# Attention stage: the seven identity-by-identity products left out of every step in which the whole pipeline runs

## The reference, cut to what matters

```python
x = x + 0.5 * ffn(layernorm(x), gate_w, w1, w2, w3)
x = x + attention(layernorm(x), Wq, Wk, Wv, Wb, conv_q_w, conv_k_w, conv_v_w, rms_w, Wo)
x = x + 0.5 * ffn(layernorm(x), gate_w, w1, w2, w3)
```

```python
A = I + tril(Kb K^T, -1);  T = inverse(A);  W = T Kb;  U = T Vb
mid = U - W S^T
O = Q S^T + (Q K^T * M) mid
S = S + mid^T K
```

## Time and profile before

| | |
|---|---|
| median of three runs | 1484.42 us |
| the profiled execution | 1485.0 us, span 1483.3 us |
| TensorE (PE) busy | 1339.8 us, 90% of the span |
| VectorE (DVE) busy | 1080.7 us, 73% |
| ScalarE (ACT) busy | 888.6 us, 60% |
| GpSimd (POOL) busy | 791.0 us, 53% |
| mean granted TensorE clock | 0.952 of 2.4 GHz |

### The profile page before, as it was taken

The page is one execution under the profiler, slowest core; times in us unless marked ns, Lnnn a source line. Parts: engine busy times, 40 slices in busy tenths (PEclk is TensorE's granted clock), DMA queues, the critical chain, the costliest instruction groups (busy, mean ns, idle before and its releaser), DMA issues. The chain is left out here.

```text
span 1483.3 us, 48601 instructions
## 1 busy us (share of the span) xinstructions
PE 1339.8 (90%) x17442; PEld 1229.8 (83%) x17442; DVE 1080.7 (73%) x3189; ACT 888.6 (60%) x2096; POOL 791.0 (53%) x1485
## 2 busy tenths in 40 slices
PE   7867999998579999999999999999999838999997
PEld 7766999998468888888878888888887628999997
DVE  6774556555577888999998998998998455555554
ACT  4434556664356777767677767677675324555663
POOL 3672333334355557567776677676866550333334
PEclk9998999999689999999999999999999768999999
DMA  9833433330011122222222222222222353333320
GB/s 265 244 123 105 124 94 94 96 89 12 22 19 42 41 51 47 66 55 75 68 65 72 58 73 75 66 73 68 67 73 47 103 175 104 100 94 91 91 76 17
DMA packets 191382, 123.11 MB, mean 83 GB/s; under 512 B 101531, under 2 KB 182951, under 8 KB 191152
## 3 DMA queue, kind: packets, MB, share of 16 engines
q1 hardware_dynamic: 167200, 77.68, 21.1%
q0 software_dynamic: 14976, 33.93, 6.6%
q10 hardware_dynamic: 8976, 8.40, 1.9%
HBM read 69.71 MB, written 57.55 MB: 86 GB/s over the span
## 5 line engine op out<-in xcount | busy, mean ns | idle before, releaser
L504 PE MATMUL ffn_both<-ws,ffn_xhi 128*128 x1472 | 252.7, 283 | 0.1
L728 DVE SCALAR_TENSOR_TENSOR ffn_hid<-ffn_both,ffn_xb,ffn_sil 128x128 f32<-128x128 f32 x368 | 103.7, 344 | 199.8 <-ACT ffn_sil L858 194.7
L1727 DVE SCALAR_TENSOR_TENSOR raw_w<-attn_raw,taps,raw_w 128x256 f32<-128x256 f32 x576 | 239.3, 482 | 4.6 <-ACT raw_w L2140 4.5
L858 ACT ACTIVATE ffn_sil<-ffn_both,ffn_xb 128x128 f32<-128x128 f32 x368 | 104.9, 368 | 189.0 <-PE ffn_both L504 189.0
L504 PEld LDWEIGHTS ffn_both<-ws,ffn_xhi 128*128 128x128 f32 x1472 | 211.1, 191 | 0.4 <-issue 0.3
L930 POOL DMA_INDIRECT out_dram<-ffn_xb,ffn_to x92 | 90.4, 983 | 167.3 <-PE ffn_both L504 112.9
L930 POOL DMA_INDIRECT x_after_first<-ffn_xb,ffn_to x92 | 90.5, 984 | 163.4 <-PE ffn_both L504 107.9
L2416 POOL TENSOR_TENSOR attn_inv<-attn_inv,attn_term 64x14 f32<-64x14 f32 (+6 forms) x448 | 138.5, 309 | 35.1
L528 PE MATMUL ffn_pos<-ws,ffn_hhi 128*128 x736 | 153.8, 292 | 2.0 <-DVE ffn_xb L741 2.0
L504 PE MATMUL ffn_both<-ws,ffn_xlo 128*128 x736 | 149.2, 285 | 0.0
L1326 PE MATMUL attn_fr<-attn_xhi,wqkv 128*128 128x256 f32 x768 | 139.9, 291 | 4.5 <-ACT attn_bth L2147 2.5
(11 more groups left out here) (333 smaller groups left out, 3532.0 us busy)
## 6 DMA issues: line engine op xcount, KB each, us to landing
ffn_xb<-listed_rows SPq DMA_DIRECT2D x184, 130.5 KB, 2.2
attn_xin<-x_after_first ACTq DMA_DIRECT2D x32, 256.0 KB, 2.7
attn_xres<-x_after_first SPq DMA_DIRECT2D x32, 256.0 KB
x_after_attention<-attn_xres SPq DMA_DIRECT2D x32, 256.0 KB
attn_xg<-x_after_attention SPq DMA_DIRECT2D x32, 256.0 KB, 3.4
ffn_xb<-in_L_attn_x_dram SPq DMA_DIRECT2D x7, 1024.0 KB, 6.7
raw_w<-in_L_ffn_w_dram SPq DMA_DIRECT2D x8, 512.0 KB, 8.8
small_blocks<-raw_w SPq DMA_DIRECT2D x256, 8.0 KB
```

What stands on the lines that cost most here:

```text
L504: last = pe.matmul(hp[k % 2][:, j, e], (xhi, xlo)[b][:, k % 2, q, j * P:(j + 1) * P], ws[:, bass.ds(experts[2 * j + e], 1), a, q].rearrang ...
L728: last = dve.scalar_tensor_tensor(hid[:, k % 2, j, e], hp[k % 2][:, j, e, HF:], xw[k % NW][:, j, DM + 3 + e:DM + 4 + e], sil[:, j, e], ALU ...
L858: last = act.activation(sil[:, j, e], hp[k % 2][:, j, e, 0:HF], ACT.Silu, scale=xw[k % NW][:, j, DM + 3 + e:DM + 4 + e])
L1727: dve.scalar_tensor_tensor(acc[:, j, r], raw[:, j, r, :, tap:tap + P], taps[:, j, r, tap:tap + 1], acc[:, j, r], ALU.mult, ALU.add)\
```

## The change

```diff
-            def x_turn(f):
+            def x_turn(f, s):
                 m = f[0]
                 wait(pe, vtok_ready, m)
-                keep_busy(fr[:, 0, 0:P], 3)
+                if not s:
+                    keep_busy(fr[:, 0, 0:P], 3)
                 pe.wait_ge(xn_ready, m + 1)
...
                 if f:
-                    x_turn(f)
+                    x_turn(f, s)
...
                 if f:
                     beta_turn(f)
-                    fill(f)
+                    if not s:
+                        fill(f)
                 if t:
                     second_products32(t)
```

## The result

The changed kernel takes 1490.67 us in the median of 20 runs (1481.31 to 1503.23) and the kernel before 1483.83 us in 20 runs of the same comparison (1477.13 to 1488.47): ratio 1.0052, 95% interval 1.0034 to 1.0069. It is slower, by about 7 us; the forecast was 1494, in the range 1482.5 to 1502.

A forecast was written before the change was run, and what follows sets the result against it. A step is bound by a closed round passing from engine to engine, not TensorE alone. 11.2 us lost to half speed less 1.5 gained is +9.7 on 1485.0, 1494.7; as a median 1494 us, range 1482.5 to 1502.

The forecast's parts named there:

- The round: Full steps: a closed round passes from engine to engine; the cut identity products stand in TensorE's two pauses.
- x_turn, 1.5 us gained: Three products before the transposes of x: 0.25 us gained in six steps behind `positions`, 0 elsewhere; bounds 0 and 4.2.
- the number forecast: Second Gram product, L1388 before the change: would wait for VectorE's L1767 in about twelve steps.
- fill, worth 0 as time: Four products before L1461: cutting leaves TensorE empty 1.2 us in each of 29 steps, no instruction earlier.
- The clock: Behind fill's pause: 3.4 us at 1.2 GHz in some steps, beginning 2 to 4 us behind L1461.
- 0.45 + 1.34 us for a fall: Extra time at half speed on L1605 (0.45) and L1614 (1.34), 1.8 us if both fell in.
- 8 falls at 1.4 us: Half-speed stretches in 8 of 29 full steps, 1.4 us each (bounds 1.0 and 1.7): 11.2 us lost.
- bounds of 4 and 14: Number of half-speed stretches in 29 steps: from one step in seven (4) to one in two (14).
- No fall: Rival: transposes and small products hold the clock at 2.4 GHz in the full steps; 1483 us, chance 0.26.
- a fall in every step: Rival: half speed behind the thin stretch in all 29 steps, +39 us, 1524 us; chance 0.06.
- The faster case: Rival: TensorE is the bound; 0.7 us from x_turn in each of 29 steps, 1464 us; chance 0.04.
- the second rival: Full steps: half speed in every one, 1524 us, as if transposes did not count for the clock; chance 0.06.

The follow-up runs named there:

- Run 1: Only the three x_turn products left out of the full steps, fill kept, against the kernel before: 1502.70 us, ratio 0.9985.
- run 2: Only the four fill products left out of the full steps, x_turn's kept, against the kernel before: 1519.69 us, ratio 1.0089.
- run 3: The changed kernel with eight identity transposes in fill's place, timed against the kernel before: 1502.59 us, ratio 0.9981.

## Why the prediction held, step by step

**The round.** Right. The cuts made no step shorter by their own length: TensorE's busy time fell by 40 us and the plain steps without a fall stayed at 23.37 us where they had 23.35 to 23.36. One reading of the round was incomplete: the prediction says that VectorE waits for L1416 and for little else, but in the same stretch it also waited 20.9 us, 23 times, for ScalarE's `squares` (L2162), nearly as long as the 22.5 us for L1416. That wait is part of the same round, and no term hangs on it.

**x_turn, 1.5 us gained.** Right in place and, within what can be told, in size. L1320 now waits for ScalarE's L2110 in 23 steps, 0.8 us at most, and L1389 waits for VectorE in 12 steps, the number forecast. The steps with `positions` at their end fell from 24.0 us or more to between 23.37 and 23.65, and the next ones rose by up to 0.25 (steps with a fall left aside). Run 1 gives the net: 2.0 us of the stretch.

**fill, worth 0 as time.** Right: 1.14 to 1.19 us of pause in most steps, no instruction earlier. The longest is 2.3 us, where a transfer was late by 1.1.

**The clock.** Right in cause and sign, not in the place within the step. The prediction had half speed begin 2 to 4 us behind L1461 and L1614 take over 2.5 us; it began 0 to 1.1 us behind, and L1615 took 1.99 to 2.68 us, over 2.5 in one of the six. What it slowed is L1606, L1507 and the small products before L1615: from L1462 to L1615 it is 3.1 to 3.5 us in these steps in place of 2.25. Of the prediction's 0.45 + 1.34 us for a fall the first came in five of the six, in whole or in part, and of the second at most half; the rest of the cost came from L1507 and the small products, which the sum had not counted.

Forecast were 8 falls at 1.4 us, 11.2 us. There were 6. The six steps with a fall, against the same kind of step without one (25.63 less 23.5, 25.01 less 23.4, 24.80 less 23.4, 25.53 less 23.7, 26.44 less 24.45, 25.24 less 23.7), took 2.1, 1.6, 1.4, 1.8, 2.0 and 1.5 us more, together 10.4. But in four of them VectorE also waited for a late transfer, 1.14, 0.23, 0.39 and 0.82 us, which is no part of the fall. Less these 2.6 us the six falls cost about 7.8 us, 1.3 each. In run 2 it was 12 falls at 1.4. So the price was near, though not by the terms that it was made of, and the number was too high by a third in one and too low by a third in the other: it was picked between bounds of 4 and 14, and that the sum came near is partly luck. The stretch adds up: 7.8 us for the falls, some 1.2 us more of late transfers than before (3.5 against 2.3), less 1.5 to 2.0 us from x_turn, gives 7.0 to 7.5, and 7.35 was measured. The median of many executions moved by 6.8 us where 9.7 was forecast.

**The rivals.** No fall, and a fall in every step: neither came, the share is 6 of 28 here and 12 of 28 in run 2. What decides in which step it comes was not found: in the changed kernel pauses of 1.45, 1.35 and 1.28 us passed without a fall and ones of 1.14 and 1.19 did not, so the length of the pause alone does not. It has a part in it: the three longest pauses, 2.29, 1.92 and 1.49 us, all had a fall, and a late transfer had lengthened each. The faster case fell with run 1. The Trainium skill's rule (TensorE: Matmul & The Clock Gate, PE-mode transpose), that transposes do not count for the clock as products do, would have given the second rival; run 3 measured it directly, and the measurement decides against it: eight transposes in the pause, no fall, and a mean clock over ten executions no lower than that of the kernel before (0.9535 against 0.9519).

## What to carry to other kernels

Before a filler product is cut, look at both of its jobs: what it delays (here nothing, since TensorE was waiting for another engine) and what it keeps (here 2.4 GHz for the dense run behind it). Here a filler in a pause was free as long as it ended before the wait did; cut one that stands where its engine is late, keep one that covers a pause between small products, and best of all fill the pause with work that has to be done anyway, then look at the granted clock again, because that work may be too thin. TensorE's busy time alone does not tell: 1.08 us on a 64x64 corner held the clock and 1.05 us on a 32x32 corner did not. And before a fall is given a price from whole steps, take out what those steps waited for other things.

## What the runs showed of the hardware that was not expected

- Products of a 64x64 and of a 32x32 corner kept TensorE busy for the same time (1.08 and 1.05 us a step); the clock held with the first (0 falls, mean clock 0.0006 below the kernel before) and not with the second (4 falls, 0.0049 below).
- Transposes of full width held the clock as products did (run 3, 0 falls).
- One stretch of 3.4 us at half speed cost a step about 1.3 us (six falls of the changed kernel, late transfers taken out) or 1.4 (run 2), less than the 1.7 us that half of it would be.
- At 1.2 GHz full-width work took 1.7 times as long (L1605 1.11 us against 0.66, L1614 3.33 against 1.99).
- The kernel before took 1484 to 1487 us in some sessions and 1505 to 1507 in others, on one chip in both, with its full steps at 664.3 and 671.4 us at the same clock of 1.00.
- In the first ffn a higher mean clock (0.96 against 0.89) bought no time, and pauses ended by nothing but issue appeared in its place.
